# Two head attentions: how the constant rows, the first operands and the causal mask of the maxima are brought in

## What is computed

```python
# b1a, relative positions, w = 128
content = einsum('bhik,bhjk->bhij', q, k) / sqrt(8)
rp = einsum('bhik,rk->bhir', q, Wr) + br
pos = take_along_axis(rp, clip(j - i, -w, w) + w, axis=-1)
out = softmax(content + pos) @ v
# b3a, rotary and causal
score = einsum('bhqd,bhkd->bhqk', rope(Q), rope(K)) / sqrt(8)
score = score - 1e10 * (1 - tril(ones))
out = softmax(score - max(score)) @ V      # then @ ow
```

## Time and profile before

| | us |
|---|---|
| median of 3 runs | 4206.79 |
| lowest, highest | 4199.53, 4208.95 |
| profiled execution | 4219.19 |
| its span | 4217.4 |
| b1a: first matmul of the projection, start of `attend`, last division | 563.31, 594.61, 1178.1 |
| b3a: the same three | 3462.74, 3505.22, 3837.1 |

### The profile page before, as it was taken

How to read it: one execution, slowest core, us unless ns; L and a number is a source line. 1 busy time by engine, 2 the same in 40 slices (tenths; PEclk the granted TensorE clock), 3 DMA queues, 4 the chain that set the end, 5 groups by cost and what they waited for, 6 DMA issues and landing times. The chain is left out here.

```text
span 4217.4 us, 100218 instructions
## 1 busy us (share of the span) xinstructions
PE 3722.3 (88%) x40681; PEld 2007.5 (48%) x40681; DVE 2758.5 (65%) x4886; ACT 2221.3 (53%) x4121; POOL 1398.7 (33%) x621
## 2 busy tenths in 40 slices
PE   7979778888859977999999999999899976998998
PEld 3344333333334434666666666666666642334335
DVE  5943457777633357787778778778787747773335
ACT  3323236777723335767676676666667623552222
POOL 3710022111100005666666666666666510000000
PEclk9979868999969988999999999999999987997999
DMA  1000037776520002322322322322222202000000
GB/s 50 0 1 0 0 112 238 232 231 225 177 86 0 0 0 49 98 60 57 95 57 62 95 57 63 93 58 71 81 62 62 52 28 79 20 23 1 0 0 11
DMA packets 168634, 283.54 MB, mean 67 GB/s; under 512 B 36253, under 2 KB 71424, under 8 KB 165736
## 3 DMA queue, kind: packets, MB, share of 16 engines
q1 hardware_dynamic: 167900, 276.87, 22.3%
q10 hardware_dynamic: 268, 0.19, 0.0%
HBM read 101.95 MB, written 74.45 MB: 42 GB/s over the span
## 5 line engine op out<-in xcount | busy, mean ns | idle before, releaser
L2183 POOL TENSOR_TENSOR b2f_norm<-b2f_norm,b2f_minus_half 128x16 f32<-128x16 f32 x192 | 555.1, 2911 | 277.1 <-DVE b2f_norm L2524 277.1
L2173 POOL TENSOR_TENSOR b2f_q<-b2f_q,b2f_q_part 128x1024 f32<-128x1024 f32 x96 | 228.1, 2376 | 850.9 <-DVE b2f_q_part L2514 850.9
L1621 ACT ACTIVATE b1a_weights<-b1a_b_ps 128x512 f32<-128x512 f32 x512 | 277.4, 597 | 39.8 <-PE b1a_b_ps L1546 37.8
L1728 DVE TENSOR_REDUCE b1a_tops<-b1a_a_ps 128x1 f32<-128x512 f32 (+3 forms) x512 | 244.4, 501 | 19.6 <-PE b1a_a_ps L1502 18.1
L1621 ACT ACTIVATE b3a_weights<-b3a_b_ps 128x512 f32<-128x512 f32 (+3 forms) x384 | 161.5, 503 | 161.6 <-PE b3a_b_ps L1556 161.5
L2523 DVE TENSOR_REDUCE b2f_norm<-xn 128x16 f32<-128x1024 f32 x192 | 234.2, 1220 | 13.6 <-ACT xn L2407 6.5
L2466 ACT ACTIVATE b2f_v_rows<-b2f_q_ps 128x1024 f32<-128x1024 f32 x96 | 98.3, 1023 | 270.1 <-DMA b2f_values<-b2f_v_rows 142.6
L2416 ACT ACTIVATE b2f_prob<-b2f_odd_ps,b2f_bias,b2f_norm 128x64 f32<-128x64 f32 x768 | 232.0, 445 | 13.5 <-DVE b2f_bias L2540 12.4
L1707 DVE TENSOR_REDUCE b3a_tops<-b3a_a_ps 128x1 f32<-128x512 f32 (+3 forms) x384 | 194.7, 553 | 67.9 <-PE b3a_a_ps L1502 65.7
L1445 POOL TENSOR_SCALAR b1a_k_op<-b1a_k_op,b1a_extra 128x1024 bf16<-128x1024 bf16 x32 | 90.6, 2842 | 433.4 <-DMA b1a_k_op<-part_copies 433.4
L2416 ACT ACTIVATE b2f_prob<-b2f_even_ps,b2f_bias,b2f_norm 128x64 f32<-128x64 f32 x768 | 231.9, 450 | 2.3 <-DVE b2f_bias L2540 2.3
(11 more groups left out here) (484 smaller groups left out, 8499.4 us busy)
## 6 DMA issues: line engine op xcount, KB each, us to landing
b2f_values<-b2f_v_rows SPq DMA_DIRECT2D x1534, 64.0 KB
position_scratch<-b1a_e_sb SPq DMA_DIRECT2D x128, 512.0 KB, 3.9
b1a_band<-position_scratch SPq DMA_DIRECT2D x128, 384.0 KB
b2f_wqkv<-in_b2f_wqkv SPq DMA_DIRECT2D x6, 1536.0 KB, 7.1
b2f_turn<-in_c_rotary SPq DMA_DIRECT2D x6, 1024.0 KB, 8.2
part_copies<-b1a_parts SPq DMA_DIRECT2D x12, 256.0 KB
b2f_wo<-in_b2f_wo SPq DMA_DIRECT2D x6, 512.0 KB, 9.5
part_copies<-b3a_parts SPq DMA_DIRECT2D x12, 256.0 KB
```

The costliest lines, as they stand in the source:

```text
L1621: act.activation(weights[:, s % P_RING, c, lo:QW], b_room(s, c)[:, lo:QW], ACT.Exp).then_inc(S.exps_ready, 1)
L1728: ins = dve.tensor_reduce(out, src, AX_X, ALU.max)
L2173: pool.tensor_tensor(G.q[:, g % 2], G.q[:, g % 2], G.q_part[:], ALU.add) \
L2183: pool.tensor_tensor(part, part, G.minus_half[:, 0:HEADS], ALU.pow) \
```

## The change

Three things, in both attentions where not said otherwise:

- The constant rows of `q_op` and `k_op` come from DRAM, as ten transfers of 16 rows each at the head of SP's queue in `project_heads`; GpSimd's two clearings and two additions go, its clearing of the `values` column stays.
- After the six copies of batch 0 have landed, SP loads the operands of groups 0 and 1 (24 transfers) in `project_heads`, ahead of the six copies of batch 1. `attend` starts without these loads and does not wait for them; groups from 2 on are loaded as before. In b3a the weights of the next stage (`fetch`) are requested after the loads of group 2, where they stood after those of group 1.
- In b3a only, `L1493` goes: the scores are formed without the mask. VectorE reduces the columns before the diagonal (none for t % 4 = 0), and a fused add and maximum takes the diagonal's 128 columns of PSUM and the mask, which VectorE has converted to f32 at the start of the stage, into a third column of `tops`. The keys' side keeps its mask.

```diff
+                for h in range(2):
+                    rows = slice(64 * h + ONES_AT, 64 * h + 64)
+                    for n in range(2):
+                        sp.dma_start(q_op[rows, n], W["c_extra_rows"][0]).then_inc(S.loaded, 16)
+                    for n in range(K_RING):
+                        sp.dma_start(k_op[rows, n, 0], W["c_extra_rows"][1]).then_inc(S.loaded, 16)
                 for b in range(B):
                     for part in range(3):
                         for i in range(2):
                             sp.wait_ge(S.rounded, 6 * b + 2 * part + i + 1)
                             sp.dma_start(K.copies[b, i, part], parts[:, b, i, part]).then_inc(S.copied, 16)
+                    if b == 0:
+                        sp.wait_ge(S.copied, 16 * 6)
+                        for g in range(EARLY):
+                            load_operand(sp, K, g, 0, q_op[:, g % 2], S.loaded)
+                            load_operand(sp, K, g, 1, k_op[:, g % K_RING, 0], S.loaded)
                 sp.wait_ge(S.copied, 16 * 6 * B)
+                sp.wait_ge(S.loaded, 16 * (2 * (2 + K_RING) + 2 * EARLY * OPERAND_LOADS))
...
-                pool.memset(q_op[:], 0.0).then_inc(S.cleared, 1)
-                pool.memset(k_op[:, :, 0], 0.0).then_inc(S.cleared, 1)
                 pool.memset(values[:, :, :, :, HD:HD + 1], 1.0).then_inc(S.ones_ready, 1)
-                pool.wait_ge(S.cleared, 2)
-                pool.tensor_scalar(q_op[:], q_op[:], extra[:, 0:1], None, ALU.add).then_inc(S.ones_ready, 1)
-                pool.tensor_scalar(k_op[:, :, 0], k_op[:, :, 0], extra[:, 1:2], None, ALU.add) \
-                    .then_inc(S.ones_ready, 1)
...
+            def wait_operand(eng, g, done):
+                if g >= EARLY:
+                    eng.wait_ge(done[g % 2], loaded(g))
...
-                    masked = not relative and t // 4 == i
-                    if masked:
-                        for at, (h, piece) in enumerate(pieces(t)):
-                            if piece == i:
-                                wait_for_a_room("tops", a, at)
-                                pe.matmul(a_room("tops", a, at)[:, cols(t % 4, P)], ident[:],
-                                          unseen[:, 0], start=True, stop=False, skip_group_check=True)
...
                         pe.matmul(a_room("tops", a, at)[:, 0:wide], q_op[rows, g % 2, cols(t, P)],
-                                  k_op[rows, g % K_RING, 0, i * QW:i * QW + wide], start=not masked,
-                                  stop=True, skip_group_check=True).then_inc(S.scores_ready, 1)
+                                  k_op[rows, g % K_RING, 0, i * QW:i * QW + wide], start=True,
+                                  stop=True).then_inc(S.scores_ready, 1)
...
-                            wide = min(QW, seen(t) - i * QW)
-                            dve.tensor_reduce(tops[:, u, i:i + 1], room[:, 0:wide], AX_X, ALU.max) \
-                                .then_inc(S.topped, 1)
+                            if t // 4 != i:
+                                dve.tensor_reduce(tops[:, u, i:i + 1], room, AX_X, ALU.max) \
+                                    .then_inc(S.topped, 1)
+                                continue
+                            if n >= 4:
+                                dve.wait_ge(S.topped, n - 3)
+                            if t % 4:
+                                chain.n += 1
+                                dve.tensor_reduce(tops[:, u, i:i + 1], room[:, 0:t % 4 * P], AX_X, ALU.max) \
+                                    .then_inc(S.dve_chain, 1)
+                            dve.tensor_tensor_reduce(summed[:, n % 4, 0:P], room[:, cols(t % 4, P)],
+                                                     later[:], 1.0, LOWEST, ALU.add, ALU.max,
+                                                     accum_out=tops[:, u, 2:3]).then_inc(S.topped, 1)
                             continue
...
-                    for g in range(GROUPS):
+                    for g in range(EARLY, GROUPS):
                         load_queries(sp, g)
                         load_keys(sp, g)
-                        if g == 1:
+                        if g == EARLY:
...
-                    for t in range(-3, STEPS + 1):
-                        if t + 3 < STEPS and (t + 3) % QT == 0:
+                    for t in range(STEPS + 1):
+                        if EARLY * QT <= t + 3 < STEPS and (t + 3) % QT == 0:
                             load_queries(sp, (t + 3) // QT)
-                        if t < 0:
-                            continue
-                        if t < STEPS and t % QT == 0:
+                        if EARLY * QT <= t < STEPS and t % QT == 0:
                             load_keys(sp, t // QT)
...
+                if not relative:
+                    chain(dve.tensor_copy(later[:], unseen[:, 0]))
```

More of the change, by code:

```diff
@@ L1123, in masked_parts, with head_attention @@
                                        op0=ALU.mult, op1=ALU.add))
-def head_attention(nc, K, weights, key, xn, x, relative, fetch=()):
+def head_attention(nc, K, W, weights, key, xn, x, relative, fetch=()):
     with ExitStack() as ctx:
@@ L1140, in head_attention @@
             position_table(nc, key, weights.positions, small, table)
-        project_heads(nc, K, weights, key, xn, weights.w, small, q_op, k_op, values, relative)
+        project_heads(nc, K, W, weights, key, xn, weights.w, small, q_op, k_op, values, relative)
         attend(nc, K, key, q_op, k_op, extra, ident, values, table, unseen, merged, relative, fetch)
@@ L1174, in _, with project_heads @@
                 chain(dve.tensor_copy(table[:], chosen[:]))
-def project_heads(nc, K, weights, key, xn, w, small, q_op, k_op, values, relative):
+def project_heads(nc, K, W, weights, key, xn, w, small, q_op, k_op, values, relative):
     with ExitStack() as ctx:
@@ L1301, with load_operand @@
 P_RING = 2
+def load_operand(eng, K, g, i, operand, done):
+    b, pair = g // PAIRS, g % PAIRS
+    copies = K.copies[b, i]
+    for h in range(2):
+        for slot, n, part in RUNS:
+            rows = slice(64 * h + HD * slot, 64 * h + HD * (slot + n))
+            at, step = (part * P * T, 0) if i == 0 else (0, P * T)
+            source = bass.AP(copies.tensor, copies.offset + at + (2 * pair + h) * HD * T,
+                             [[step, n], [T, HD], [1, T]])
+            eng.dma_start(operand[rows], source).then_inc(done, 16)
 def attend(nc, K, key, q_op, k_op, extra, ident, values, table, unseen, merged, relative,
@@ L1374, in attend @@
         o_ps = M.ps(f"{key}_o_ps", [P, QW])
+        summed = M.sb(f"{key}_summed", [P, 4, BAND if relative else P])
+        later = None if relative else M.sb(f"{key}_later", [P, P])
         if relative:
@@ L1389, in attend @@
             queries, keys = (S.queries_even, S.queries_odd), (S.keys_even, S.keys_odd)
-            OPERAND_LOADS = 2 * len(RUNS)
             def loaded(g):
-                return 16 * OPERAND_LOADS * (g // 2 + 1)
-            def load_operand(sp, g, i, operand, done):
-                b, pair = g // PAIRS, g % PAIRS
-                copies = K.copies[b, i]
-                for h in range(2):
-                    for slot, n, part in RUNS:
-                        rows = slice(64 * h + HD * slot, 64 * h + HD * (slot + n))
-                        at, step = (part * P * T, 0) if i == 0 else (0, P * T)
-                        source = bass.AP(copies.tensor, copies.offset + at + (2 * pair + h) * HD * T,
-                                         [[step, n], [T, HD], [1, T]])
-                        sp.dma_start(operand[rows], source).then_inc(done, 16)
+                return 16 * OPERAND_LOADS * ((g - EARLY) // 2 + 1)
+            def wait_operand(eng, g, done):
+                if g >= EARLY:
+                    eng.wait_ge(done[g % 2], loaded(g))
             def load_queries(sp, g):
-                if g >= 2:
-                    sp.wait_ge(S.less_ready, half * (g - 1))
-                    sp.wait_ge(queries[g % 2], loaded(g - 2))
-                load_operand(sp, g, 0, q_op[:, g % 2], queries[g % 2])
+                sp.wait_ge(S.less_ready, half * (g - 1))
+                wait_operand(sp, g - 2, queries)
+                load_operand(sp, K, g, 0, q_op[:, g % 2], queries[g % 2])
             def load_keys(sp, g):
@@ L2869, in build @@
             layer_norm(nc, K, "n1", x, xn, fetch=fetch)
-            head_attention(nc, K, w, "b1a", xn, x, relative=True)
+            head_attention(nc, K, W, w, "b1a", xn, x, relative=True)
         with ExitStack() as own:
@@ L2880, in build @@
             layer_norm(nc, K, "n3", x, xn, fetch=fetch)
-            head_attention(nc, K, w, "b3a", xn, x, relative=False, fetch=fetch_later)
+            head_attention(nc, K, W, w, "b3a", xn, x, relative=False, fetch=fetch_later)
             block3_ffn(nc, K, f, xn, x)
```

27 lines of the change are left out of this document (13 added, 14 removed).

## The result

| | before | after |
|---|---|---|
| median, five runs each, in turns on one chip (us) | 4199.53 (4189.91 to 4208.95) | 4166.77 (4159.12 to 4167.43) |
| profiled execution (us) | 4219.19 | 4166.77 |
| ratio, with its 95% interval | | 0.9912 (0.9896 to 0.9928) |

The account below looks back on a forecast made before the run. Each group of heads was taken to be paced by TensorE, with VectorE close behind. Terms of 4.7 (b1a), 11.2 (b3a's start) and 9.6 us (mask), 25.5 together, off 4206.79 gave 4181.3; own range 4174 to 4188, wide range 4163 to 4198.

Parts of the forecast that it names:

- GpSimd's rows: Projections of b1a and b3a: without GpSimd's additions blocking VectorE, 7.3 and 8.0 us come back; the ten transfers cost nothing.
- b1a's start: First position product of b1a's `attend`: 0.4 us earlier, between -0.9 and +1.5, as SP's queue takes nearly all of 7.3.
- b3a's first maximum: Start of b3a's `attend`: no wait for operands, so VectorE's first maximum comes 11.2 us earlier, bounds 12.5, 10.2 and 6.
- b1a's group 0: First group of b1a: without group 1's loads between band transfers, 4.3 of 4.76 us of VectorE's idle go, bounds 1 and 6.
- rival D: Copies land late behind loads, b1a's bands stay DMA-bound: b1a gains 0, b3a's start 6, mask 9.6; 4191 us, chance 0.10.
- The mask: b3a's groups: mask matmuls leave TensorE, VectorE adds the mask; 0.6 us a group, 9.6 over 16 groups, bounds 28 and -16.
- ticks 0 to 2: b3a's groups, where TensorE is late: up to three pairs of mask matmuls (0.66 us) come back, net 0.2 to 0.4.
- Tick 3's pair: b3a's groups: removing tick 3's two mask matmuls gives nothing, as the key scores behind them wait for ScalarE's exponentials.
- ticks 4 to 7: b3a's groups: four pairs of mask matmuls give back 0.88 us, VectorE's additions take 0.5, net 0.4.
- A: b3a, ticks 4 to 7: VectorE's additions eat what TensorE frees, mask term 0 instead of 9.6; 4191 us, chance 0.18.
- B: b3a: all of the mask is on TensorE's path, 28 us in place of 9.6; 4163 us, chance 0.10.
- C: b3a: VectorE becomes the bound, held by the fused instruction and its read; 1.4 us a group more; 4213 us, chance 0.04.

Follow-up runs that it names:

- mask_early: The changed kernel with the mask on VectorE only in ticks 0 to 3 of a group, on TensorE in the others; ratio 0.9931 to before.
- loads_only: The changed kernel with the mask on TensorE as before, keeping the constant rows by transfers and the early operand loads; ratio 0.9954 to before.
- pe_kept_old: The changed kernel with TensorE still doing the mask matmuls in their old place, overwritten by the scores; ratio 0.9949 to before.

## Why the prediction was right in kind and short in size

- GpSimd's rows, right. The operations run at the forecast pace, and the loads start 14.98 us after the first matmul where 15.1 was forecast. The landing of batch 0's last copy, taken as 2.2 us without a row for the 0.6 us of barrier in it, took 2.0 (575.1 to 577.15).
- b1a's start, forecast 0.4 earlier, measured 0.9 later; b3a's first maximum, forecast 11.2, measured 10.7. One term was wrong in both: what lies around the six copies. Their transfer takes the forecast 5 us, but 7.7 to 8.3 us pass from the first issue to the next stage's first instruction where I had 6.8 to 6.9. I had split the 2.8 us of a lone copy into about 1.0 of transfer and 1.8 of the rest, and had no term for the thin rest of traffic behind the burst.
- b1a's group 0, right: 4.7 and, in the second traces, 3.7 for 4.3. The DMA engines did not keep a part of the idle (rival D). That the stretch gained 5.0 for a forecast 4.7 is luck in part: the start lost 0.9 where 0.4 was to be gained, and the step to group 1, not forecast, gave 1.7.
- The mask, **the step that failed**: "In ticks 0 to 2 TensorE is late, so up to three pairs (0.66) come back, less the 0.16 that tick 1 adds while VectorE is dense, and less what the last wait keeps: I take 0.2 to 0.4." `mask_early` has 0.64. There the waits of ticks 1 to 4 fell by 1.0 us, more than the 0.66 of three pairs, and VectorE's additions took 0.4 of it; nothing was deducted for a last wait. Of the forecast's 0.2 to 0.4 the sum used the low end; the high end would have made 12.8 us instead of 9.6. "Tick 3's pair ... gives nothing" belongs to the same step: `mask_early` takes four pairs off TensorE (0.88 us), not three, and no run has tick 3's alone. For ticks 4 to 7 the forecast 0.4 stands against 0.34. With 1.0 a group instead of 0.6 the term is 15 us by the period; in the stretch it is 12.9 behind the early loads and 15.6 without them, in place of 9.6.
- Group starts, not forecast: 1.1 of the 12.5 us of the loads in b3a are not in the first maximum. They lie in the first group's period, 17.9 us in `loads_only` and 18.9 in before. With the mask moved too that period is 19.3 and 19.1 us, so the whole change does not keep them.
- The merges, not forecast at all: 3.4 us by the traces (1.2 and 2.2). The kernel that only adds a clearing is 4.6 us faster (1 to 8) and has the same short merges. "Later stages are unchanged" was true of the code, and not of the clock that they get. The change earned this by where it put the merges, not by what it does.
- Rivals. A (nothing back for the mask, a period of 19.1) and B (all of it, 17.3) fall to the period of 18.1. C falls too: a fused operation of 283 ns with its read delays the next by 0.20 us, and VectorE's additions cost 0.4 us a group. The Trainium skill (VectorE: DVE Perf Modes, The DRAIN you can't avoid) has the next operation wait for an empty pipe, and adds that one that is not held starts earlier; the starts here, closer together than the duration, agree with the second.

Of 37 us, 30.3 lie in the attentions where 25.5 were forecast and 3.4 in the merges. The other 3.3 are within what the measurement leaves open (30 to 44).

## What to carry to other kernels

When work leaves the engine that paces a loop, do not discount its yield wait by wait: take the queue time that goes from the pacing engine, less the work that the other engine gains, over a whole group. Here that is 1.76 - 0.8 = 1.0 us, as measured. The other engine's waits over the group are the bound (3.5 us here). It is the sum of one case, and `pe_kept_old` splits it otherwise (1.4 of relief less 0.4 of work). And compare stretches, since a few microseconds of any change can come from where the clock's fall meets the next short stage; a kernel that only shifts the phase helps to tell the two apart.

## What the runs showed of the hardware

- The same merge takes 3.5 or 5.2 us after b1a, and 6.9 or up to 9.9 after b3a, by where the granted clock falls. The kernel before has the longer ones, and with one more VectorE clearing of 0.91 us in each projection it has the shorter ones.
- Two matmuls of 64 rows in different halves, one behind the other in the queue, take the 0.23 us of one. A 128-row matmul between them ends that: with the same instructions a group takes 19.9 us against 19.5, and TensorE is busy for all of it.
- Six 256 KB copies behind a queue of small loads move at up to 387 GB/s for 1 us, but 7.7 to 8.3 us pass from their first issue to the next stage; in b1a the last 2 us with traffic carry only 22 to 60 GB/s.
